# Conditioned residual convolution and expert mixing on one core: order of the opening loads, filler matmuls and the last unit's stores

## The chip, the cores and the metric

The kernel runs on one core of one Trainium2 chip. The metric is device time in microseconds of one execution; shown are the median and the limits of three runs. A profiled execution comes apart from these, with its own time and its span, which is the stretch from its first to its last recorded work.

## The reference, cut to what matters

```python
# x: (128, 64, 1024), cond_128: (128, 128)
def _L0_cond_ref(x, c, weight, c_weight, bias):
    ...
    out = lax.conv_general_dilated(x, weight, window_strides=(STRIDE,), padding=[(PAD, PAD)], dimension_numbers=('NCH', 'OIH', 'NCH'), feature_group_count=GROUPS)
    ctx = jnp.einsum('nd,od->no', c, c_weight)
    out = out + ctx[:, :, None] + bias[None, :, None]
    return out

def _L1_cond_ref(x, embedding, W0, b0, W1, b1, W2, b2, weight, bias_k):
    ...
    h = jax.nn.gelu(embedding @ W0 + b0, approximate=False)
    h = jax.nn.gelu(h @ W1 + b1, approximate=False)
    att = jax.nn.softmax((h @ W2 + b2) / T, axis=-1)
    agg_w = jnp.einsum('bk,koi->boi', att, weight[..., 0])
    agg_b = att @ bias_k
    out = jnp.einsum('boi,bih->boh', agg_w, x) + agg_b[:, :, None]
    return out
x = x + _L0_cond_ref(x, cond_128, L0_cond_weight, L0_cond_c_weight, fside_S_0)
x = x + _L1_cond_ref(x, cond_128, L1_cond_W0, L1_cond_b0, L1_cond_W1, L1_cond_b1, L1_cond_W2, L1_cond_b2, L1_cond_weight, L1_cond_bias_k)
```

Per sample: a grouped convolution of 9 taps over 64 channels with a residual, then a 64 x 64 matrix of its own, a softmax mixture of 8 expert matrices, again with a residual. Both residuals are folded into the matrices (the identity is added to them), all constants into one bias per sample and channel.

## The kernel before, in words

The 128 samples are worked in 16 units of 8 (NU, S). A unit u passes five stages.

- **Load.** SP and ScalarE each issue four DMAs (`load`, L195 and L285), one for each half of the length, into `xin[u % 2]`. Both queues run on the same 16 data engines.
- **Turn in.** VectorE transposes `xin` to `xph` (`turn_in`, L402), counted by `turned`. Unit 1 is turned in two parts (`second_phases`), with unit 0's first two column turns between them.
- **Convolution.** TensorE, `conv` (L528): four groups g, 12 matmuls each, into one half of PSUM tensor `yps`. Group 0 waits for `turned`, group g of unit 0 from g = 2 on for column turn g - 2 (`ycol_made`).
- **Turn back.** VectorE takes each group out of PSUM (`y_columns`, L424), and after four of them makes `ynat` (`y_natural`, L433).
- **Mixing.** TensorE, `mix` (L551): four pairs of samples o, into `zps`; ScalarE evacuates each with its bias (`evacuate`, L303) to `zout`, SP stores it (`store`, L199). `matrices` (L312) makes the unit's 64 x 64 matrices on ScalarE from `mixt`.

TensorE does unit u's groups 0 and 1, the pairs 0 and 1 of unit u - 1, groups 2 and 3, pairs 2 and 3. Every engine runs its own list in order; semaphores join them.

**The opening.** Inputs beside x: `mlps` (233.5 KB, all of the small network), `shares` (107 KB, identity and index patterns), `consts` (160 KB), `wraw` (208 KB, convolution), `mixw` (128 KB, experts). TensorE runs the network on 128 samples: L636 (first layer, h1 follows as Gelu on ScalarE, L328), L637 (for the bias), L639 (second layer, h2, L331), L642 and L643 (logits). VectorE takes the maximum, ScalarE exp (L333, which needs another function table than Gelu), GpSimd makes `att` (L247). L647 transposes it, ScalarE scales it four times (`attt`, L340). The aggregates (L509, 16 matmuls) mix the experts; they wait for `mixw` with GpSimd's identity added (L254, `mix_eye`). ScalarE's `gather` (L317) takes them out, four times. L623 makes the constants of the experts and waits for the first gather. conv(0) waits for two gathers, for `turned`, and for `w_sum`: `wraw` is doubled to the other 64 partitions (L443, VectorE, `w_both`), then GpSimd adds the residual (L257).

Between these steps TensorE multiplies a zeroed tile, a filler whose result nobody reads (`keep_on(n)`, L608; a matmul of it shows as two records): 4 at the very start, 3 ahead of L647, 3 ahead of the aggregates, 3 ahead of conv(0).

**The last unit.** Its group 3 is convolved in two halves of samples (`conv_last`, L565), turned back by quarters (L475, L482), each counted by `last_cols` and `last_nat`. Then `mix_first` (L577) makes pairs 0 and 2 whole, `mix_half` (L588) pairs 1 and 3 by halves of the length, ScalarE evacuates the first two in two instructions each (L379) and two halves (L385), VectorE the other two halves (L498). SP stores the two whole pairs (L226, 512 KB) and four halves (L229, 256 KB).

Of the kernel before, what the change touches and what calls it, by code (L numbers as in the profile page):

```python
# [42 lines left out]
def build(nc, x, conv_w, mlp, share, const_w, mix_w, out):  # L43
    ctx = ExitStack()
    with ctx:
# [725 lines left out]
```

## Time and profile before

| what | us |
|---|---|
| median of three runs | 248.84 |
| lowest, highest | 248.31, 249.13 |
| the profiled execution | 249.11 |
| its span | 247.3 |

| engine | busy us | share of the span |
|---|---|---|
| TensorE, matmul | 237.3 | 96% |
| VectorE | 220.3 | 89% |
| ScalarE | 126.6 | 51% |
| GpSimd | 10.4 | 4% |

All times in the profile are counted from the start of the span; the profiled execution took 1.8 us more than its span. DMA moved 68.39 MB, 277 GB/s on average. A row of the timeline gives start, duration, engine, line, operation, what is written from what is read, the count, and in brackets how long the engine stood idle before it and what released it. PE is TensorE's matmul, PEld its weight load, DVE is VectorE, ACT ScalarE, POOL GpSimd; SPq and ACTq are the issue of DMAs by SP and ScalarE.

### The profile page before, as it was taken

To read this page: it belongs to the slowest core of one execution; us is meant where nothing else is said; L and a number is where in the kernel's file an instruction comes from. 1 tells how busy PE (TensorE), PEld (TensorE's weight loads), DVE (VectorE), ACT (ScalarE), POOL (GpSimd) and SP (SyncE) were. 2 spreads that over 40 slices of the span, in tenths; PEclk is the share of its full clock that TensorE was granted. 3 is DMA by queue.
4 is the path that set the end of the run, shared out by engine and by line. 5 is a ranking of instruction groups with operands and counts; after the bars stand their busy time and mean duration, and the time that the engine had idled before them with its cause. 6 is when DMAs were issued, how large, how long until landed. Compare 5 with 4: busy or idle time off the path is not lost.

```text
span 247.3 us, 5763 instructions
## 1 busy us (share of the span) xinstructions
PE 237.3 (96%) x2162; PEld 103.9 (42%) x2162; DVE 220.3 (89%) x113; ACT 126.6 (51%) x208; POOL 10.4 (4%) x36
## 2 busy tenths in 40 slices
PE   6799999999999999999999999999999999999991
PEld 4643334344344444444444444444444444444530
DVE  1075899999999999999999999999999999999582
ACT  2457007374535456383645445373745446263772
POOL 1325000000000000000000000000000000000000
PEclk9689999999999999999999999999999999999999
DMA  7998566999999999999999999999999997444448
GB/s 189 307 326 240 152 125 191 258 312 365 357 322 268 359 263 383 249 380 238 334 294 292 327 256 378 247 388 239 362 273 322 298 281 293 170 170 172 171 184 328
DMA packets 28555, 68.39 MB, mean 277 GB/s; under 512 B 3184, under 2 KB 3568, under 8 KB 28544
## 3 DMA queue, kind: packets, MB, share of 16 engines
q1 hardware_dynamic: 19104, 50.98, 62.3%
q10 hardware_dynamic: 9440, 17.26, 26.5%
q8 instruction: 7, 0.11, 0.2%
q14 instruction: 4, 0.03, 0.0%
HBM read 34.67 MB, written 33.55 MB: 276 GB/s over the span
## 4 chain that ended last, share of the span: by engine, by line
PE 91%; DVE 3%; ACTq 2%; ACT 1%; issue 1%; DVEq 0%
PE yps L528 64%; PE zps L551 21%; PE yps L608 3%; DVE ynat L433 2%; ACTq L285 2%; PE yps L565 1%; PE zps L577 1%; DVE ycol L424 1%; PE yps L509 0%; PE yps L623 0%; PE yps L588 0%; ACT mixt L317 0%; DVE xin L498 0%; PE zps L588 0%; ACT L324 0%
## 5 line engine op out<-in xcount | busy, mean ns | idle before, releaser
L528 PE MATMUL yps<-xph,wraw 64*64 64x512 f32 x1512 | 169.0, 589 | 0.0
L303 ACT ACTIVATE zout<-zps,gamu 128x512 f32<-128x512 f32 x120 | 72.7, 688 | 95.3 <-PE zps L551 75.6
L528 PEld LDWEIGHTS yps<-xph,wraw 64*64 64x64 f32 x1512 | 67.5, 132 | 94.0 <-issue 94.0
L424 DVE STREAM_TRANSPOSE ycol<-yps 128x1024 f32<-128x1024 f32 x63 | 75.2, 1224 | 7.0 <-PE yps L528 5.4
L402 DVE STREAM_TRANSPOSE xph<-xin 128x4160 f32<-128x4160 f32 (+2 forms) x17 | 71.7, 4220 | 5.1 <-DMA xin<-in_x 5.1
L433 DVE STREAM_TRANSPOSE ynat<-ycol 128x4096 f32<-128x4096 f32 x15 | 66.7, 4446 | 1.1
L551 PE MATMUL zps<-ynat,mixv 64*64 64x512 f32 x480 | 57.8, 589 | 0.3 <-DVE ynat L433 0.3
L312 ACT ACTIVATE mixv<-mixt 64x256 f32 (+1 forms) x64 | 42.4, 663 | 1.4 <-ACT mixt L317 0.2
L551 PEld LDWEIGHTS zps<-ynat,mixv 64*64 64x64 f32 x480 | 21.6, 133 | 29.9 <-issue 29.6
L608 PE MATMUL yps<-zout 128*128 128x256 f32 x26 | 10.4, 566 | 1.3 <-POOL zout L243 1.3
L241 POOL COPY gamu<-gam 128x4 f32 (+1 forms) x16 | 2.9, 188 | 199.9 <-ACT zout L303 191.8
L608 PEld LDWEIGHTS yps<-zout 128*128 128x128 f32 x26 | 7.3, 296 | 3.2 <-POOL zout L243 1.3
L482 DVE STREAM_TRANSPOSE ynat<-ycol 128x1024 f32<-128x1024 f32 x4 | 4.7, 1224 | 0.1
L445 DVE TENSOR_REDUCE negmax<-zps 128x1 f32<-128x8 f32 x1 | 0.2, 167 | 4.0 <-PE zps L643 4.0
L351 ACT ACTIVATE gam<-zps 128x64 f32<-128x64 f32 x1 | 0.2, 224 | 6.8 <-PE zps L630 6.8
L324 ACT ACT_TABLE_LOAD x1 | 1.3, 1283 | 4.7 <-issue 4.7
L443 DVE COPY wraw<-wraw 64x832 f32<-64x832 f32 x1 | 0.6, 586 | 3.0 <-DMA wraw<-in_conv_w 3.0
L317 ACT ACTIVATE mixt<-yps 128x1024 f32<-128x1024 f32 x2 | 1.9, 1021 | 2.3 <-PE yps L509 2.3
L379 ACT ACTIVATE xin<-zps,gamu 128x512 f32<-128x512 f32 x4 | 2.4, 688 | 1.4 <-PE zps L577 1.4
L565 PE MATMUL yps<-xph,wraw 64*64 64x256 f32 x48 | 3.0, 375 | 0.0
L565 PEld LDWEIGHTS yps<-xph,wraw 64*64 64x64 f32 x48 | 2.2, 132 | 1.2 <-issue 1.0
L340 ACT ACTIVATE zout<-zps,shares 128x128 f32<-128x128 f32 x4 | 1.1, 368 | 2.5 <-PE zps L647 2.5
(56 smaller groups left out, 34.8 us busy)
## 6 DMA issues: line engine op xcount, KB each, us to landing
out<-zout SPq DMA_DIRECT2D x60, 512.0 KB, 6.2
xin<-in_x SPq DMA_DIRECT2D x64, 258.0 KB, 7.2
xin<-in_x ACTq DMA_DIRECT2D x64, 258.0 KB, 7.4
out<-xin SPq DMA_DIRECT2D x2, 512.0 KB, 2.7
out<-xin SPq DMA_DIRECT2D x4, 256.0 KB, 3.0
mlps<-in_mlp SPq DMA_DIRECT2D x1, 233.5 KB, 2.8
wraw<-in_conv_w ACTq DMA_DIRECT2D x1, 208.0 KB, 3.7
zout<-in_const_w SPq DMA_DIRECT2D x1, 160.0 KB, 9.3
```

The costliest lines, as they stand in the source:

```text
L241: nc.gpsimd.tensor_copy(gamu[slot][:], gam[:, bass.ds(PR * u, PR)]).then_inc(gam_cut, 1)
L285: act.dma_start(*x_piece(slot, u, 1, k, t)).then_inc(x_in[slot], 16)
L303: nc.scalar.activation(zout[:, o].rearrange("p (i c j q) -> p c i j q", i=2, c=2, q=PH)[:, c], zps[:, at:at + BANK].rearrange("p (q i j) - ...
L312: nc.scalar.activation(mix_places(slot, h, d), mix_values(u, d), ACT.Copy).then_inc(mixv_made, 1)
L402: nc.vector.transpose(xph[slot][:, :, :, at:to].rearrange("q g s j t -> q j s g t"), xin[slot][:, :, PH * at:PH * to].rearrange("q c (j p) ...
L424: nc.vector.transpose(ycol[:, :, :, :, :, g].rearrange("p i s j q c -> p (i s j) q c"), yps[:, 2 * BANK * (g % 2):2 * BANK * (g % 2) + 2 * ...
L433: nc.vector.transpose(ynat[slot][:].rearrange("p t q i s (j l) -> p (i s j) q t l", l=16), ycol[:].rearrange("p i s j q g c -> p (i s j q ...
L482: nc.vector.transpose(ynat[1][:, :, :, i, 2 * sh:2 * sh + 2].rearrange("p t q s (j l) -> p (s j) q t l", l=16), ycol[:, i, 2 * sh:2 * sh + ...
L528: last = nc.tensor.matmul(yps[C * c:C * c + C, at:at + BANK].rearrange("p (s f) -> p s f", s=S // 2), wsum[rows, b, g], xph[slot][rows, g, ...
L551: last = nc.tensor.matmul(zps[C * s:C * s + C, at:at + BANK].rearrange("p (n j) -> p n j", j=NJ), mixv[slot][rows, 2 * o + s], ynat[slot][ ...
L565: last = nc.tensor.matmul(y_last(sh)[C * c:C * c + C, i].rearrange("p (s f) -> p s f", s=2), wsum[rows, b, G - 1], xph[1][rows, G - 1, 2 * ...
L608: nc.tensor.matmul(yps[:, 3 * BANK:3 * BANK + BANK // 2], still[:, 0:P], still[:, 0:BANK // 2], start=True, stop=True)
```

## The change

- SP no longer issues `shares`; ScalarE does, as its first DMA. `wraw` and `mixw` are issued by ScalarE behind h1 instead of ahead of x(0), `mixw` first. The Gelu table and the warm-up instruction stand ahead of load(0). Of x(1)'s four pieces on ScalarE two are issued behind h1, two behind `beta`.
- The copy of `wraw` to the other partitions goes from VectorE to ScalarE, behind `attt` and ahead of the first gather. GpSimd adds the constants' identity ahead of the sum over `wraw`.
- Filler: one matmul behind L637 and one behind L639 are added, the three ahead of the aggregates become five, the three ahead of conv(0) go.
- The last unit is mixed, evacuated and stored in eight halves of a pair, in the order of a table, `LAST`. ScalarE evacuates six, VectorE two.

```diff
+LAST = (0, 0), (2, 0), (0, 1), (2, 1), (1, 0), (3, 0), (1, 1), (3, 1)
...
         def z_half(o, i):
 
-            return (yps, zps)[i][:, BANK * (o - 1):BANK * (o - 1) + 2 * BANK].rearrange(
-                "p (c h f) -> p h c f", c=2, h=2)[:, 0]
+            bank, at = {(0, 0): (zps, 0), (2, 0): (yps, 2), (0, 1): (zps, 2), (2, 1): (zps, 0),
+                        (1, 0): (yps, 0), (3, 0): (yps, 2), (1, 1): (zps, 2), (3, 1): (zps, 0)}[o, i]
+            return bank[:, BANK * at:BANK * at + 2 * BANK].rearrange("p (c h f) -> p h c f", c=2, h=2)[:, 0]
...
             sp.dma_start(mlps[:], mlp).then_inc(mlp_in, 16)
-            sp.dma_start(shares[:], share).then_inc(share_in, 16)
             load(0, 0)
...
-            for o in (0, 2):
-                sp.wait_ge(z_act, o + 2)
-                sp.dma_start(z_rows(NU - 1, o), out_last(o)).then_inc(z_out[o], 16)
-            for o, i, made, n in ((1, 0, z_act, 5), (1, 1, z_dve, 1), (3, 0, z_act, 6), (3, 1, z_dve, 2)):
-                sp.wait_ge(made, n)
+            for n, (o, i) in enumerate(LAST):
+                sp.wait_ge(z_act if n < 6 else z_dve, n % 6 + 1)
                 sp.dma_start(z_rows(NU - 1, o)[:, H * i:H * i + H], out_half(o, i)).then_inc(z_out[o], 16)
...
-            pool.wait_ge(w_both, 1)
-            nc.gpsimd.tensor_tensor(wsum[:, 1], wsum[:, 1], wraw[:, NT * G:].broadcast_to([P, G, C]),
-                                    ALU.add).then_inc(w_sum, 1)
             pool.wait_ge(const_in, 16)
...
+            pool.wait_ge(w_both, 1)
+            nc.gpsimd.tensor_tensor(wsum[:, 1], wsum[:, 1], wraw[:, NT * G:].broadcast_to([P, G, C]),
+                                    ALU.add).then_inc(w_sum, 1)
...
-            act.dma_start(wraw[0:C], conv_w).then_inc(w_in, 16)
-            act.dma_start(mixw, mix_w).then_inc(mix_in, 16)
-            load(0, 0)
+            act.dma_start(shares[:], share).then_inc(share_in, 16)
             act.wait_ge(zeroed, 1)
             nc.scalar.activation(warm[:], warm[:], ACT.Gelu)
-            load_block(1, 1, 0)
+            load(0, 0)
             act.wait_ge(mlp_in, 16)
             act.wait_ge(mm, 1)
             nc.scalar.activation(h1, sps[:, 0:NS], ACT.Gelu, bias=b0s).then_inc(act_mlp, 1)
-            load_block(1, 1, 1)
+            act.dma_start(mixw, mix_w).then_inc(mix_in, 16)
+            act.dma_start(wraw[0:C], conv_w).then_inc(w_in, 16)
+            load_block(1, 1, 0)
...
+            load_block(1, 1, 1)
             act.wait_ge(share_in, 16)
             act.wait_ge(mm, 4)
             for o in range(RO):
                 nc.scalar.activation(attt[:, o], sps[:, 0:NS], ACT.Copy, scale=turn[:, o:o + 1]).then_inc(soft, 1)
+
+            act.wait_ge(w_in, 16)
+            nc.scalar.activation(wraw[C:P], wraw[0:C], ACT.Copy).then_inc(w_both, 1)
             gather(0, 1, 4)
...
-            dve.wait_ge(w_in, 16)
-            nc.vector.tensor_copy(wraw[C:P], wraw[0:C]).then_inc(w_both, 1)
...
             nc.tensor.matmul(gps[0:C, 0:NS], cws, condt, start=True, stop=True).then_inc(beta_mm, 1)
+            keep_on(1)
             pe.wait_ge(act_mlp, 1)
             nc.tensor.matmul(sps[:, NS:2 * NS], w1s, h1, start=True, stop=True).then_inc(mm, 1)
+            keep_on(1)
...
             keep_on(3)
+            keep_on(2)
             aggregates()
             output_constants()
-            keep_on(3)
...
             pe.wait_ge(mixv_made, 4 * NU)
+            pe.wait_ge(last_nat, 1)
+
+            pe.wait_ge(z_made, 8 * NU - 10)
+            mix_half(0, 0)
+
+            pe.wait_ge(last_cols, 2)
+            mix_half(2, 0)
             pe.wait_ge(last_nat, 2)
 
-            pe.wait_ge(z_made, 8 * NU - 10)
-            mix_first(0)
-
             pe.wait_ge(z_made, 8 * NU - 8)
-            mix_first(2)
+            mix_half(0, 1)
+
+            pe.wait_ge(z_act, 1)
+            mix_half(2, 1)
             pe.wait_ge(last_nat, 3)
-
             pe.wait_ge(last_cols, 4)
             mix_half(1, 0)
+            pe.wait_ge(z_act, 2)
             mix_half(3, 0)
             pe.wait_ge(last_nat, 4)
-
-            pe.wait_ge(z_act, 2)
+            pe.wait_ge(z_act, 3)
             mix_half(1, 1)
-
             pe.wait_ge(z_act, 4)
             mix_half(3, 1)
```

ScalarE's list in the opening: as it was, up to `beta`, and as it is now, from load(0), which stands behind `shares`, the table and the warm-up, to the copy of `wraw` (the first zout activation is h1, the second h2, the four are attt):

```order
L320 DMA wraw<-in_conv_w 64x832
L321 DMA zout<-in_mix_w 128x256
L285 DMA xin<-in_x 16x8x516 x4
L324 ACT_TABLE_LOAD
L324 ACTIVATE warm<-warm 128x1
L285 DMA xin<-in_x 16x8x516 x2
L328 ACTIVATE zout<-zps,mlps 128x128
L285 DMA xin<-in_x 16x8x516 x2
L331 ACTIVATE zout<-zps,mlps 128x128
L333 ACT_TABLE_LOAD
L333 ACTIVATE expv,esum<-zps,negmax 128x8
L336 ACTIVATE beta<-zps,mlps 64x128
```

```order
L280 DMA xin<-in_x 16x8x516 x4
L321 ACTIVATE zout<-zps,mlps 128x128
L322 DMA zout<-in_mix_w 128x256
L323 DMA wraw<-in_conv_w 64x832
L280 DMA xin<-in_x 16x8x516 x2
L326 ACTIVATE zout<-zps,mlps 128x128
L328 ACT_TABLE_LOAD
L328 ACTIVATE expv,esum<-zps,negmax 128x8
L331 ACTIVATE beta<-zps,mlps 64x128
L280 DMA xin<-in_x 16x8x516 x2
L336 ACTIVATE zout<-zps,shares 128x128 x4
L339 ACTIVATE wraw<-wraw 64x832
```

h1 has no table load right ahead of it any more, and four DMA issues stand between h1 and h2 where two stood. The copy of `wraw` is new, ahead of gather.

TensorE's list up to the first convolutions, before and now (yps<-zout 128x256 is the filler, the 64x512 rows are the aggregates, yps<-zout,beta is L623):

```order
L636 MATMUL zps<-mlps 128x128
L637 MATMUL zps<-mlps 64x128
L639 MATMUL zps<-zout,mlps 128x128
L642 MATMUL zps<-mlps,zout 128x8
L643 MATMUL zps<-mlps,ones 128x8
L608 MATMUL yps<-zout 128x256 x3
L647 MATMUL zps<-shares,att 128x128
L608 MATMUL yps<-zout 128x256 x3
L509 MATMUL yps<-zout 64x512 x8
L509 MATMUL zps<-zout 64x512 x8
L623 MATMUL yps<-zout,beta 128x512
L608 MATMUL yps<-zout 128x256 x3
```

```order
L612 MATMUL zps<-mlps 64x128
L583 MATMUL yps<-zout 128x256
L615 MATMUL zps<-zout,mlps 128x128
L583 MATMUL yps<-zout 128x256
L619 MATMUL zps<-mlps,zout 128x8
L620 MATMUL zps<-mlps,ones 128x8
L583 MATMUL yps<-zout 128x256 x3
L624 MATMUL zps<-shares,att 128x128
L583 MATMUL yps<-zout 128x256 x5
L495 MATMUL yps<-zout 64x512 x8
L495 MATMUL zps<-zout 64x512 x8
L598 MATMUL yps<-zout,beta 128x512
```

The filler moved from the place ahead of the convolution to places between the network's layers and ahead of the aggregates.

## Rows read from the trace of the kernel before

**Rows 1.** The page's chain, by engine.

```profile
PE 91%; DVE 3%; ACTq 2%; ACT 1%; issue 1%; DVEq 0%
```

**Rows 2.** The chain in order of time, the start: start us, us, what.

```profile
9.01 2.86 PE yps L608 x6
...
19.43 10.52 PE yps L528 x96
...
35.85 1.95 PE zps L551 x16
```

**Rows 3.** Slices of 1 us, the opening, from 6 us on.

```profile
core 0: us, PE busy (x) PEld busy (x) DVE busy (x) ACT busy (x) POOL busy (x), PEclk, DMA share, GB/s
...
6.00:7.00 1.00, 0.47 (x2) 0.30 (x2) 0.00 (x0) 0.48 (x2) 0.00 (x0) 1.00 0.97 281
...
7.00:8.00 1.00, 0.10 (x2) 0.11 (x1) 0.00 (x0) 0.57 (x2) 0.00 (x0) 0.80 1.07 287
...
8.00:9.00 1.00, 1.00 (x5) 0.95 (x5) 0.00 (x0) 1.00 (x1) 0.00 (x0) 0.50 1.07 235
...
14.00:15.00 1.00, 1.00 (x10) 0.36 (x17) 1.00 (x1) 0.00 (x0) 0.91 (x1) 0.79 1.05 349
```

**Rows 4.** Timeline of the opening.

```profile
4.54 0.38 PE L636 MATMUL zps<-mlps 128*128 128x128 f32 x2
...
4.67 1.28 ACT L324 ACT_TABLE_LOAD   x1 [4.67 <-issue]
...
6.12 1.24 ACTq L285 DMA_DIRECT2D xin<-in_x  x2
...
7.41 0.37 ACT L331 ACTIVATE zout<-zps,mlps 128x128 f32<-128x128 f32 x1 [0.93 <-PE zps L639]
...
9.90 0.60 POOL L247 TENSOR_SCALAR att<-expv,erec 128x128 f32<-128x128 f32 x1 [8.48 <-DVE erec L447]
...
13.64 1.27 POOL L261 TENSOR_TENSOR zout<-zout,shares 64x512 f32<-64x512 f32 x1 [1.74 <-DMA zout<-in_const_w]
...
17.04 1.10 PE L623 MATMUL yps<-zout,beta 80*128 80x512 f32 x2 [0.43 <-ACT mixt L317]
...
17.97 1.46 PE L608 MATMUL yps<-zout 128*128 128x256 f32 x6
...
18.67 1.02 ACT L317 ACTIVATE mixt<-zps 128x1024 f32<-128x1024 f32 x1
```

**Rows 5.** Timeline of VectorE, 12 to 37 us.

```profile
13.03 4.51 DVE L402 STREAM_TRANSPOSE xph<-xin 128x4160 f32<-128x4160 f32 x1 [3.23 <-DMA xin<-in_x]
...
19.37 2.38 DVE L402 STREAM_TRANSPOSE xph<-xin 128x2112 f32<-128x2112 f32 x1 [1.83 <-DMA xin<-in_x]
...
22.24 1.25 DVE L424 STREAM_TRANSPOSE ycol<-yps 128x1024 f32<-128x1024 f32 x1 [0.49 <-PE yps L528]
```

**Rows 6.** Issues of x by ScalarE at 3.96 and 4.73, and at 6.74.

```profile
xin<-in_x ACTq DMA_DIRECT2D x2, 258.0 KB, 9.3
...
xin<-in_x ACTq DMA_DIRECT2D x1, 258.0 KB, 12.2
```

**Rows 7.** The tail: timeline, a slice of 1 us, the landing of L229's stores.

```profile
235.15 2.37 DVE L482 STREAM_TRANSPOSE ynat<-ycol 128x1024 f32<-128x1024 f32 x2
...
237.62 1.95 PE L577 MATMUL zps<-ynat,mixv 64*64 64x512 f32 x16 [0.47 <-issue]
...
238.85 2.42 ACT L379 ACTIVATE xin<-zps,gamu 128x512 f32<-128x512 f32 x4 [1.38 <-PE zps L577]
...
240.15 1.49 SPq L226 DMA_DIRECT2D out<-xin  x2
...
240.00:241.00 1.00, 0.97 (x20) 0.36 (x12) 0.59 (x1) 1.00 (x3) 0.00 (x0) 1.00 0.05 20
...
241.88 2.56 SPq L229 DMA_DIRECT2D out<-xin  x4
...
DMA to landing us min/median/max: 2.9/3.0/3.2
```

More of the change, by code:

```diff
@@ L159, in y_last @@
                 "p (i h f) -> p h i f", i=2, h=2)[:, 0]
-        def z_first(o):
-            return zps[:, BANK * o:BANK * o + 2 * BANK].rearrange("p (c f) -> p c f", c=2)
         def z_half(o, i):
-            return (yps, zps)[i][:, BANK * (o - 1):BANK * (o - 1) + 2 * BANK].rearrange(
-                "p (c h f) -> p h c f", c=2, h=2)[:, 0]
+            bank, at = {(0, 0): (zps, 0), (2, 0): (yps, 2), (0, 1): (zps, 2), (2, 1): (zps, 0),
+                        (1, 0): (yps, 0), (3, 0): (yps, 2), (1, 1): (zps, 2), (3, 1): (zps, 0)}[o, i]
+            return bank[:, BANK * at:BANK * at + 2 * BANK].rearrange("p (c h f) -> p h c f", c=2, h=2)[:, 0]
         def out_last(o):
@@ L223, in _ @@
                     store(u, o)
-            for o in (0, 2):
-                sp.wait_ge(z_act, o + 2)
-                sp.dma_start(z_rows(NU - 1, o), out_last(o)).then_inc(z_out[o], 16)
-            for o, i, made, n in ((1, 0, z_act, 5), (1, 1, z_dve, 1), (3, 0, z_act, 6), (3, 1, z_dve, 2)):
-                sp.wait_ge(made, n)
+            for n, (o, i) in enumerate(LAST):
+                sp.wait_ge(z_act if n < 6 else z_dve, n % 6 + 1)
                 sp.dma_start(z_rows(NU - 1, o)[:, H * i:H * i + H], out_half(o, i)).then_inc(z_out[o], 16)
             for o in range(PR):
-                sp.wait_ge(z_out[o], 16 * NU + 16 * (o % 2))
+                sp.wait_ge(z_out[o], 16 * NU + 16)
         @block.gpsimd
@@ L376, in _ @@
             act.wait_ge(turned, NU)
-            def evacuate_first(o, c):
-                nc.scalar.activation(
-                    out_last(o).rearrange("p (i c j q) -> p c i j q", i=2, c=2, q=PH)[:, c],
-                    z_first(o)[:, c].rearrange("p (q i j) -> p i j q", q=PH, i=2),
-                    ACT.Identity, bias=gamu[1][:, o:o + 1]).then_inc(z_act, 1)
             def evacuate_half(o, i):
@@ L388, in evacuate_half @@
                     ACT.Identity, bias=gamu[1][:, o:o + 1]).then_inc(z_act, 1)
-            for o in (0, 2):
-                act.wait_ge(last_mixes, 1 + o // 2)
-                for c in range(2):
-                    evacuate_first(o, c)
-            for o in (1, 3):
-                act.wait_ge(last_mixes, 3 + o // 2)
-                evacuate_half(o, 0)
+            for n, (o, i) in enumerate(LAST[:6]):
+                act.wait_ge(last_mixes, n + 1)
+                evacuate_half(o, i)
         @block.vector
@@ L495, in _ @@
             dve.wait_ge(gam_cut, NU)
-            for n, o in enumerate((1, 3)):
-                dve.wait_ge(last_mixes, 5 + n)
+            for n, (o, i) in enumerate(LAST[6:]):
+                dve.wait_ge(last_mixes, 7 + n)
                 nc.vector.tensor_scalar(
-                    out_half(o, 1).rearrange("p (c j q) -> p c j q", c=2, q=PH),
-                    z_half(o, 1).rearrange("p c (q j) -> p c j q", q=PH),
+                    out_half(o, i).rearrange("p (c j q) -> p c j q", c=2, q=PH),
+                    z_half(o, i).rearrange("p c (q j) -> p c j q", q=PH),
                     gamu[1][:, o:o + 1], None, ALU.add).then_inc(z_dve, 1)
@@ L570, in conv_last @@
                 last.then_inc(last_conv, 1)
-            def mix_first(o):
-                for c in range(2):
-                    rows = slice(C * c, C * c + C)
-                    for s in range(2):
-                        last = nc.tensor.matmul(
-                            z_first(o)[C * s:C * s + C, c].rearrange("p (n j) -> p n j", j=NJ), mixv[1][rows, 2 * o + s],
-                            ynat[1][rows, o // 2, :, :, s].rearrange("p q i j -> p (q i) j"),
-                            start=True, stop=True)
-                last.then_inc(last_mixes, 1)
             def mix_half(o, i):
@@ L589, in mix_half @@
                             z_half(o, i)[C * s:C * s + C, c].rearrange("p (n j) -> p n j", j=NJ),
-                            mixv[1][rows, 2 * o + s], ynat[1][rows, o // 2, :, i, 2 + s],
+                            mixv[1][rows, 2 * o + s], ynat[1][rows, o // 2, :, i, 2 * (o % 2) + s],
                             start=True, stop=True)
```

## The prediction

> **What bounds the kernel now.** I read the page's chain first [rows 1]: 91% of it is TensorE, so what counts is when TensorE's unbroken stretch begins and what follows it. The chain in order of time [rows 2] gives the beginning: the first convolution starts at 19.43 us, unit 0's four groups run 10.52, so 2.63 each, and the first mixing is at 35.85. From there TensorE alternates without a gap, and a shift of 35.85 shifts everything behind it. So the change has two parts: the start, up to 35.85, and the tail behind the last mixing.
>
> In the start three things end close together. First TensorE's own time filler, L608: it is on the chain at 9.01 for 2.86 us, and it runs from 17.97 to 19.43, straight ahead of conv(0). The early ones ran at half clock: six filler records took 2.86 then and 1.46 at the end [rows 2, 4]. The granted clock is 1.00 in the slice from 6, 0.80 in that from 7, 0.50 in that from 8 and 0.79 in that from 14, which puts the fall at 7.6 and the rise at 14.4; TensorE was busy 0.47 and 0.10 of the two slices at the fall [rows 3]. Second, VectorE turns x of unit 0 from 13.03 for 4.51 us, on the arrival of its last piece. Third, it turns x of unit 1 from 19.37, again on the arrival [rows 5].
>
> **The start, edit by edit.**
> *Order of transfers.* On ScalarE's queue wraw (208 KB) and mixw (128 KB) stood ahead of x(0); now only the shares (107 KB) do, 229 KB less. Pieces of 258 KB landed on this queue at 3.96 + 8.9 = 12.9 us (the 9.3 of the row is the median of two issues, the other landing later) and, four pieces on, at 6.74 + 12.2 = 18.9: 1.5 us each, about 170 KB/us [rows 6]. So x(0) lands 1.4 earlier, 11.6 instead of 13.0, and its turn ends at about 16.1 instead of 17.5. Mixw then lands near 12.3 and wraw near 13.6; SP's const_w, which GpSimd took up at 13.64 [rows 4], comes some 0.6 earlier. The bytes up to the end of x(1) are the same, and the data engines moved 235 to 349 GB/s throughout [rows 3], so x(1) hardly moves: the two queues are better balanced, and I take 19.2 for 19.37.
>
> *Gelu table first.* The load (1.28 us at 4.67) ended at 5.95 while the matmul for h1 was through at 4.92 [rows 4]. It now runs from 1.35, and h1 can begin at 5.0 instead of 6.1. But behind h1 ScalarE's queue now issues mixw, wraw and two pieces of x before it comes to h2. Two pieces took 1.24 [rows 4], so four issues take 2.5, and h2 starts at 7.6; before it was 7.41 [rows 4]. **The table's gain is given back to four DMA issues**: this edit alone is worth 0 to -0.2.
>
> *Filler.* One matmul of it now stands behind L637 and one behind L639, both where TensorE would wait; three stay ahead of L647, five replace three ahead of the aggregates, none stands ahead of conv(0). What this costs hangs on the clock. **If it stays full** (case A): from the end of h2 to the filler it was 1.2 us (7.78 to 9.01), at full clock some 0.3 less, but exp waits for its table until 7.97 + 1.28 = 9.3 anyway, where before it was 9.25. Att was made at 10.50 [rows 4] and is again, L647 is through at 11.0, and five fillers, ten records at 0.243, end at 13.4. By then ScalarE's four attt (each like h2's 0.37, so 1.5 at most) and mixw with GpSimd's adds (12.3 and under 1 us: att took it 0.60 for as many elements) are ready. The aggregates start at 13.4 instead of 14.65, the end of the fillers before. From there to the end of L623 it was 3.5, up to 18.14 [rows 4], and nothing follows it now, so conv(0) can start at 16.9. **If it falls at 7.6 as before** (case B): the fillers ahead of L647 end at 12.1, five more begin at 12.5, four records run at 0.47 until 14.4, six at 0.243, and the aggregates start at 15.9, 1.2 later: conv(0) at 19.3, a gain of 0.1.
>
> *The copy of wraw from VectorE to ScalarE, behind attt.* ScalarE has no row for 64x832: between h2's 0.37 for 128 elements a partition and 1.02 for 1024 [rows 4], and by the length near 0.88. It runs from 13.6 to 14.5, just ahead of gather, whose matmuls are then through at 14.6: hidden by them, with 0.1 to spare. A wraw that lands later pushes gather and conv(0) one for one. GpSimd's constant add now comes first (1.27, done by 14.4), then its sum over wraw (under 1 us, by 15.4): hidden until 16.9.
>
> *What is late next.* Group 2 of conv(0) needs the first column turn, which VectorE does behind x(1): 19.2 + 2.38 + 1.25 [rows 5] and two handovers, 23.0. Before, group 2 began at 19.43 + 5.26 = 24.69. So the gain is capped at 1.7, and reached if conv(0) starts by 17.7: case A has 0.8 to spare. From group 2 to the mixing it was 11.2, and the order there is the old one: mixing at 34.2.
>
> **The tail.** Before, the first mixing of the last unit waits for both halves of ynat (235.15 + 2.37) and takes 1.95 for two pairs; ScalarE starts at 238.85, and the first store issues at 240.15, behind two evacuations. The data engines are nearly empty from 240 to 241 (20 GB/s), and the last four stores issue from 241.88 over 2.56 us, the last at 243.8 and landing 3.0 later at 246.9 [rows 7]. About 2.1 MB are to be written behind 240.9; at 5.4 us for them, which is 385 GB/s, data end at 246.3, so this is bound by bandwidth. Now the first step is half a pair (1.95 / 4, 0.5 us). It needs ynat's first half (236.4) and TensorE, which is free at 237.15 (0.47 idle before 237.62). ScalarE starts at 237.9, each evacuation 0.61, the first store issues at 238.65 and seven more 0.64 apart, to 243.2. The last half of ynat is made at 240.6, the last pair at 241.7, and VectorE's two evacuations are ahead of SP's turn for them. The data engines are busy with the unit before until 239.75, then have 2.1 MB without a break: 5.5 us, to 245.2 instead of 246.3, **1.05 earlier**. By issue and landing it is 243.2 + 3.0 = 246.2 instead of 246.9, 0.7. I take 1.05, since the engines' bandwidth is the nearer bound, and keep 0.6 to 1.3.
>
> The Trainium skill (DMA: Bandwidth & Descriptors, Anatomy of one DMA) gives a DMA some 2.0 us fixed plus its bytes at 436 GB/s, fitted on GpSimd's path: 2.6 us for a half. By it, as an estimate, 243.2 + 2.6 would give 1.1 for the tail; the trace's 3.0 gives 0.7.
>
> **Sum.** Case A: 1.7 + 1.05 = 2.75. The profiled execution took 249.11, 0.27 over the median of 248.84; against the median it is 246.1. Case B: 0.1 + 1.05, that is 247.7.
>
> **Rivals.**
> *B, the clock falls anyway.* For it: the two fillers still leave TensorE idle from 6.7 to 8.0. Against: the gap ahead of L639 is closed. 247.7.
> *C, the gap freed ahead of conv(0) costs the clock (slower).* Without the last fillers TensorE idles around L623, and if the clock then falls, conv(0) runs at half rate. The one fall in the trace lasted 6.8 us, 3.4 us of work. From A's 16.9 group 2 then begins at 25.6, which the tail makes even; from B's 19.3 at 28.0, 3.3 late, less 1.05: 251.1. It decides where the clock is 0.50 from 19 us on. Against it: TensorE idled 0.43 ahead of L623 before [rows 4] and the clock held.
> The Trainium skill (TensorE: Matmul & The Clock Gate, What's actually happening) calls throttled the default that activity releases; by it filler taken out is a risk, and the fall at 7.6 agrees.
> *D, wraw comes late.* It is now the last of the matrices on ScalarE's queue, and its copy holds gather. At 15 us conv(0) starts at 18, at 16.5 at 19.4, and the start's gain is gone: 247.8. The steady landing rate speaks against it.
> *E, the tail gives nothing,* if half rows are slower to write or the issues bind: A becomes 247.1, B 248.7, no change.
> *F, x(1) comes later than before,* since its last two pieces are issued only behind exp, at 9.6: at 20.1 A becomes 247.0. The queue has work until 15, so I give it little.
>
> **How the numbers follow.** A 0.45 (246.1), B 0.28 (247.7), D 0.07 and F 0.05 (247 to 247.8), E 0.09 (half of it no change), C 0.06. The likeliest is A, 246.2 with 0.1 for small handovers. The range goes from A with a tail of 1.3 and x(1) 0.4 earlier, 245.4, to B with a tail of 0.6, 248.2. A measurement of this kernel can tell 0.3% from no change, 0.75 us, so faster means under 248.1: A, D, F, most of B and half of E, 0.82; no change 0.12; slower 0.06.
>
> **What would show it.** For A: granted clock 1.00 from 8 to 13 us, aggregates at 13.4, conv(0) at 16.9, its group 2 at 23.0 straight behind the first column turn, mixing at 34.2. In every case h2 at 7.6, right behind the issues. In the tail: stores 0.64 apart and no empty slice in the data engines. If h2 comes before 7.2 or conv(0) after 19.4, my account of the start is wrong; if, measured from the last unit's mixing, data end less than 0.6 earlier, that of the tail is.

## The result and the profile after

The changed kernel takes **250.53 us** (median of 18 runs, 249.04 to 252.40) where the kernel before, run beside it, takes 248.64. The ratio is 1.008, interval 1.006 to 1.010: **slower by 1.9 us**. The forecast was 246.2 with a range up to 248.2, so it was wrong, in sign too. The profiled execution took 250.66, against 249.11 before: 1.55 us more. In some sets one execution stands far apart (422.17 us among the 18 of the kernel before, 644.53 among the twelve of t6 below), and the ratios leave it out.

The page's chain answers to [rows 1]: TensorE has fallen from 91% to 84%, and 5% of the path is now a load of x.

```profile
PE 84%; DVE 6%; DMA 5%; ACTq 1%; ACT 1%; issue 0%; DVEq 0%; POOL 0%; POOLq 0%
```

The chain in order of time (start, us, what) answers to [rows 2] and says which load:

```profile
10.15 13.26 DMA xin<-in_x
...
23.43 2.38 DVE xph L391
25.81 1.14 DVE ycol L413
...
27.09 5.42 PE yps L514 x48
...
33.82 4.46 DVE ynat L422
...
38.41 1.95 PE zps L537 x16
```

ScalarE's last piece of x(1), issued at 10.15, lands at 23.4. Its turn in, the first column turn and conv(0)'s group 2 follow without a gap, and the first mixing stands at 38.41 where it was 35.85. That is 2.56 us lost in the start. From there the order is the old one.

The timeline of the opening answers to [rows 4, 5]:

```profile
5.62 0.37 ACT L321 ACTIVATE zout<-zps,mlps 128x128 f32<-128x128 f32 x1 [2.95 <-PE zps L611]
...
6.63 1.42 ACTq L280 DMA_DIRECT2D xin<-in_x  x2
8.10 0.37 ACT L326 ACTIVATE zout<-zps,mlps 128x128 f32<-128x128 f32 x1 [2.12 <-issue]
...
11.48 2.32 PE L583 MATMUL yps<-zout 128*128 128x256 f32 x10
16.90 1.12 PE L495 MATMUL yps<-zout 32*64 32x512 f32 x16 [3.10 <-POOL zout L249]
...
20.30 5.39 PE L514 MATMUL yps<-xph,wraw 64*64 64x512 f32 x48
27.09 5.39 PE L514 MATMUL yps<-xph,wraw 64*64 64x512 f32 x48 [1.40 <-DVE ycol L413]
...
14.30 4.51 DVE L391 STREAM_TRANSPOSE xph<-xin 128x4160 f32<-128x4160 f32 x1 [3.97 <-DMA xin<-in_x]
23.43 2.38 DVE L391 STREAM_TRANSPOSE xph<-xin 128x2112 f32<-128x2112 f32 x1 [4.62 <-DMA xin<-in_x]
...
16.00 0.76 POOL L249 TENSOR_TENSOR zout<-zout,shares 128x16 f32<-128x16 f32 x4 [4.96 <-DMA zout<-in_mix_w]
...
17.18 0.90 ACT L339 ACTIVATE wraw<-wraw 64x832 f32<-64x832 f32 x1 [4.30 <-DMA wraw<-in_conv_w]
```

Every load on ScalarE's queue behind x(0)'s third piece lands later than forecast: x(0) is complete at 14.3, mixw at 15.8 (GpSimd waits 4.96 us for it), wraw at 17.1 (ScalarE waits 4.30), x(1) at 23.4. The matrices were not issued late: mixw and wraw were issued at 5.6 and 6.0 and landed 10.2 and 11.1 us on. The last piece of x(1) was, at 10.15 instead of 6.74; run t7 below tests that. The issues of x(0)'s third and fourth piece by ScalarE, 2.85 and 3.5 us into the span, in the view of DMAs (KB, us to landing), answer to [rows 6]:

```profile
xin<-in_x ACTq DMA_DIRECT2D x1, 258.0 KB, 7.7
...
xin<-in_x ACTq DMA_DIRECT2D x1, 258.0 KB, 10.7
```

That is 10.5 and 14.2, a step of 3.7 us where the two steps before are 2.0 and 1.6. The slices of 1 us (columns as in [rows 3]) show the data engines at that time:

```profile
10.00:11.00 1.00, 0.78 (x4) 0.35 (x2) 0.16 (x1) 0.39 (x3) 0.56 (x1) 1.00 1.05 324
11.00:12.00 1.00, 0.81 (x5) 0.79 (x6) 0.00 (x0) 0.26 (x1) 0.04 (x1) 1.00 1.09 246
12.00:13.00 1.00, 1.00 (x7) 0.87 (x6) 0.00 (x0) 0.89 (x4) 0.00 (x0) 1.00 1.12 220
13.00:14.00 1.00, 0.81 (x4) 0.38 (x2) 0.00 (x0) 0.00 (x0) 0.00 (x0) 1.00 1.06 211
14.00:15.00 1.00, 0.00 (x0) 0.00 (x0) 0.70 (x1) 0.00 (x0) 0.00 (x0) 1.00 1.05 205
...
19.00:20.00 1.00, 0.72 (x2) 0.30 (x2) 0.00 (x0) 1.00 (x2) 0.00 (x0) 1.00 1.07 225
```

The last two columns are the share in which the data engines were busy, and what they moved. The share stays at 1.05 to 1.12 whether they move 324 or 205 GB/s: **a full share is not a full rate**. Before, the same slices were these, with the fourth in [rows 3]:

```profile
11.00:12.00 1.00, 1.00 (x5) 0.82 (x4) 0.00 (x0) 0.00 (x0) 0.91 (x3) 0.50 1.07 352
12.00:13.00 1.00, 1.00 (x5) 0.82 (x4) 0.00 (x0) 0.61 (x3) 0.00 (x0) 0.50 1.08 291
13.00:14.00 1.00, 1.00 (x4) 0.82 (x3) 0.97 (x1) 0.53 (x3) 0.35 (x1) 0.50 1.04 324
```

So the four slices from 11 us moved 352, 291, 324 and 349 GB/s, and now move 246, 220, 211 and 205, which is 0.43 MB less. From 19 to 20 ScalarE's queue runs all but alone, 0.20 of 0.22 MB, at 225. In the changed kernel the granted clock (the column before the share) is 1.00 in all of these.

The tail, timeline and slices, answers to [rows 7]:

```profile
240.78 2.37 DVE L468 STREAM_TRANSPOSE ynat<-ycol 128x1024 f32<-128x1024 f32 x2
...
240.99 4.95 SPq L224 DMA_DIRECT2D out<-xin  x8
...
242.08 1.09 PE L563 MATMUL yps<-ynat,mixv 64*64 64x256 f32 x16 [0.40 <-DVE ynat L468]
```

```profile
240.00:241.00 1.00, 1.00 (x20) 0.49 (x12) 0.97 (x4) 0.76 (x3) 0.00 (x0) 1.00 0.99 401
...
245.00:246.00 1.00, 0.00 (x0) 0.00 (x0) 0.42 (x1) 0.00 (x0) 0.00 (x0) 1.00 1.00 371
...
247.00:248.00 1.00, 0.00 (x0) 0.00 (x0) 0.00 (x0) 0.00 (x0) 0.00 (x0) 0.95 0.84 320
```

From 240 us on the data engines no longer pause: they write 371 to 406 GB/s in every full slice, until 247.85. The old end, 246.3, moved by the 2.56 of the start would be 248.86: the tail gives 1.0 us. And 2.56 - 1.0 is the 1.55 between the profiled executions.

### The profile page after: what moved, and what is told of

It reads as the page before. It is cut to its first block, busy times and chain, and to the rows that moved or that the text cites. A ratio compares the mean times of both kernels' runs of the same rounds, so it can differ in the third digit from the quotient of the medians.

```text
span 248.9 us, 5802 instructions
## 1 busy us (share of the span) xinstructions
PE 235.6 (95%) x2180; PEld 103.2 (41%) x2180; DVE 219.4 (88%) x112; ACT 127.6 (51%) x209; POOL 10.5 (4%) x36
## 4 chain that ended last, share of the span: by engine, by line
PE 84%; DVE 6%; DMA 5%; ACTq 1%; ACT 1%; issue 0%; DVEq 0%; POOL 0%; POOLq 0%
PE yps L514 61%; PE zps L537 20%; DMA xin<-in_x 5%; DVE ynat L422 2%; PE yps L583 2%; DVE ynat L468 1%; DVE ycol L413 1%; DVE xph L391 1%; ACTq L280 1%; DVE ycol L461 1%; PE yps L551 1%; ACT L328 1%; PE yps L563 0%; DVE xin L484 0%; PE zps L563 0%
## 5 line engine op out<-in xcount | busy, mean ns | idle before, releaser
L583 PE MATMUL yps<-zout 128*128 128x256 f32 x28 | 9.0, 465 | 1.3 <-POOL zout L238 1.3
L583 PEld LDWEIGHTS yps<-zout 128*128 128x128 f32 x28 | 6.0, 230 | 2.3 <-POOL zout L238 1.3
L495 PE MATMUL yps<-zout 32*64 32x512 f32 x16 | 1.1, 611 | 3.1 <-POOL zout L249 3.1
L339 ACT ACTIVATE wraw<-wraw 64x832 f32<-64x832 f32 x1 | 0.9, 896 | 4.3 <-DMA wraw<-in_conv_w 4.3
L563 PE MATMUL zps<-ynat,mixv 64*64 64x256 f32 x40 | 3.0, 386 | 0.0
L484 DVE TENSOR_SCALAR xin<-zps,gamu 128x512 f32<-128x512 f32 x2 | 1.4, 746 | 0.9 <-PE zps L563 0.9
L563 PE MATMUL yps<-ynat,mixv 64*64 64x256 f32 x24 | 1.7, 384 | 0.4 <-DVE ynat L468 0.4
## 6 DMA issues: line engine op xcount, KB each, us to landing
wraw<-in_conv_w ACTq DMA_DIRECT2D x1, 208.0 KB, 11.1
zout<-in_mix_w ACTq DMA_DIRECT2D x1, 128.0 KB, 10.2
```

What stands on the lines that cost most here:

```text
L563: last = nc.tensor.matmul(z_half(o, i)[C * s:C * s + C, c].rearrange("p (n j) -> p n j", j=NJ), mixv[1][rows, 2 * o + s], ynat[1][rows, o ...
L583: nc.tensor.matmul(yps[:, 3 * BANK:3 * BANK + BANK // 2], still[:, 0:P], still[:, 0:BANK // 2], start=True, stop=True)
```

## The experiments

These were the theories before the first run. **Place**: the matrices now stand in the midst of x on ScalarE's queue, and what is behind them lands late. **Issue**: ScalarE issues them too late. **Clock**: some executions lose TensorE's clock in the new idle stretches. Ratios are to the kernel before on the same chip, whose median was 248.8.

### The parts of the change

t1 is the kernel before with the changed last unit alone. 

> The kernel before with the changed tail alone (eight halves of a pair); its opening is the old one. In the changed kernel the data end 1.0 us earlier, measured from the last unit's third turn back (L468 at 240.78 there, L482 at 238.22 before), so both theories of the start expect 247.6 +-0.2 here. A tail that gives nothing would leave 248.6; then the loss of the start would be only about 1.9 us instead of 2.9.

Measured 247.84, ratio 0.997 (0.9954 to 0.9986). The tail is a gain of 0.3 to 1.1 us.

t2 is the changed kernel with the old last unit. 

> The changed kernel with the old tail. If the two parts add, the opening costs 250.5 - 248.6 + 1.0 = 2.9 us, and this runs 251.5, with runs spread over some 3 us as those of the changed kernel are. x of unit 1 should be turned from about 23 us, as in the changed kernel's profile (23.43), not from 19.4. If it came out near 248.6 the loss would sit in the tail or in both together.

Measured 252.07, 1.012 (1.011 to 1.014): the start alone costs 3.3 us. In its profile, which is of the slowest of its five runs (254.84), x(0) is complete at 15.07, x(1) at 24.16, and the clock is lost besides (0.50 from 17 to 27 us).

t3 is t1 with the changed filler too, every load and ScalarE's list as before:

```diff
+            keep_on(1)
             pe.wait_ge(act_mlp, 1)
...
+            keep_on(1)
...
             keep_on(3)
+            keep_on(2)
             aggregates()
             output_constants()
-            keep_on(3)
```

> The kernel before with the changed filler matmuls and the changed tail; the order of all loads, the function table and the copy of wraw stay as they were. Both theories of the loads (place of the small matrices; late issue of x(1)'s last pieces) expect x(1) at 19.4 here. With the clock held at full, TensorE's aggregates start by 13.5 instead of 14.65, conv(0) waits for the turn of x(0) at 17.6, group 2 starts at 23.1 instead of 24.7: 247.6 - 1.6 = 246.0. If the clock falls at 7.6 as before, conv(0) is at 19.3 and the time 247.5. If the lost filler costs the clock at conv(0), over 249.

Measured 247.66 (247.37 to 248.18), 0.9948 (0.9934 to 0.9963); the clock is 1.00 from the start. My case A for the filler holds, yet it is worth only 0.2 beyond t1, and their intervals overlap, since conv(0) cannot use it. Its timeline:

```profile
13.27 1.11 PE L495 MATMUL yps<-zout 32*64 32x512 f32 x16
...
18.11 5.39 PE L514 MATMUL yps<-xph,wraw 64*64 64x512 f32 x48 [1.34 <-DVE xph L388]
24.18 5.39 PE L514 MATMUL yps<-xph,wraw 64*64 64x512 f32 x48 [0.68 <-DVE ycol L410]
```

Aggregates come at 13.27 (the forecast's 13.4), but conv(0) then waits for x(0)'s turn in, group 2 for x(1)'s. TensorE is no longer what binds the start; x is. And x varies from one execution to another: with the same loads in the same order x(1) is turned from 19.37 in the profile of the kernel before, 20.14 in t1's and 20.52 here. In the changed kernel's order of loads it is 22.63 in t8's profile, 23.43 in its own and 24.16 in t2's. So a difference in x(1) of 1.5 us or less between two profiles shows little.

### Place or issue

t4 is the changed kernel with both matrices back ahead of load(0), behind the shares:

```diff
             act.dma_start(shares[:], share).then_inc(share_in, 16)
+            act.dma_start(mixw, mix_w).then_inc(mix_in, 16)
+            act.dma_start(wraw[0:C], conv_w).then_inc(w_in, 16)
...
-            act.dma_start(mixw, mix_w).then_inc(mix_in, 16)
-            act.dma_start(wraw[0:C], conv_w).then_inc(w_in, 16)
             load_block(1, 1, 0)
```

> The changed kernel with mixw and wraw issued ahead of load(0) again (behind the shares and the table); x(1)'s last two pieces are still issued only behind exp. Theory place: the slow stretch of the data engines at 11 to 15 us (205 to 246 GB/s) comes from the matrices' rows in the midst of x, and goes with them: x(1) back at 19.4 to 20, conv(0) at 17.7, total 246 to 246.5. Theory late issue: x(1) stays at 22 to 23 because two pieces are issued at 9.5 and 10.2, total 249 to 250.5.

Measured 250.50, 1.0062 (1.0039 to 1.0085): by the time alone, no cure, and what the theory of late issue had forecast. Its timeline says otherwise:

```profile
20.31 2.38 DVE L391 STREAM_TRANSPOSE xph<-xin 128x2112 f32<-128x2112 f32 x1 [1.09 <-DMA xin<-in_x]
...
19.47 12.24 PE L514 MATMUL yps<-xph,wraw 64*64 64x512 f32 x96 [2.89 <-DVE xph L391]
```

x(1) is complete 3.1 us earlier than in the changed kernel, and the slices of 14 to 18 us move 361 to 365 GB/s: **the place of the two matrices was the cause of the late x(1)**. x(0) is no earlier than in the changed kernel (turned from 14.70 instead of 14.30). TensorE idles 2.89 us ahead of conv(0), which waits for that turn, and then the clock falls:

```profile
20.00:21.00 1.00, 1.00 (x14) 0.36 (x10) 0.69 (x1) 0.00 (x0) 0.83 (x3) 0.81 0.16 45
21.00:22.00 1.00, 1.00 (x12) 0.47 (x8) 1.00 (x1) 0.00 (x0) 0.00 (x0) 0.50 0.96 293
...
23.00:24.00 1.00, 1.00 (x8) 0.33 (x4) 0.17 (x1) 0.97 (x2) 0.00 (x0) 0.50 0.96 213
```

u1 is t4 with that gap filled, six matmuls of filler ahead of conv(0)'s wait:

```diff
+            keep_on(6)
             pe.wait_ge(w_sum, 1)
```

> The kernel with both matrices ahead of load(0), and six filler matmuls (12 records at 0.243, 2.9 us) put back ahead of conv(0), where its profile shows TensorE idle for 2.89 us and the granted clock at half from 19.6 us. If the clock is what that kernel lost after its x(1) came back at 20.3, conv(0) starts at 19.4 at full clock, the granted clock over the span is 0.997 or more, and the time 248.2 to 248.8 instead of 250.5. If the clock is no cause it stays within 0.3 of 250.5.

Measured 248.28 (248.06 to 248.74), 0.9976 (0.9963 to 0.9989). The timeline has no fall:

```profile
19.39 10.54 PE L514 MATMUL yps<-xph,wraw 64*64 64x512 f32 x96 [0.61 <-DVE xph L391]
```

All 96 matmuls take 10.54 us, where they took 12.24 in t4. So what t4 gained by its loads, some 2.2 us, it had lost again to the clock, by rival C's mechanism: an idle stretch ahead of conv(0). It takes both edits to gain it: the matrices' place alone gives 250.50 (t4), more filler in the changed kernel alone 250.44 (t8 below), place and filler together 248.28.

t5 puts wraw alone ahead of load(0), t6 mixw alone. 

> The changed kernel with wraw alone back ahead of load(0) on ScalarE's queue; mixw stays behind h1, between x(0) and x(1). Theory place, wraw's part: the 3.7 us between the third and the fourth piece of x(0) (10.5 and 14.2 in the changed kernel, 1.6 apart elsewhere) and the slow stretch come from wraw; they go, mixw lands by 14, x(1) is at 20. Theory place, mixw's part: the gap stays at 3 us or more, mixw lands at 15 to 16 and x(1) at 22 to 23. In both the time depends on the clock as well: below 249.5 if mixw lands by 14, 250 to 251 otherwise.

> The mirror image: mixw back ahead of load(0), wraw behind h1. Theory wraw's part: the gap ahead of the fourth piece of x(0) stays at 3 us, wraw lands at 16 to 17, gather and conv(0) follow it, x(1) is at 22 to 23 and the time 250 to 251. Theory mixw's part: no gap, wraw lands at 14, x(1) at 20, time below 249.5. The aggregates start at 13.4 in either case, since mixw is there.

t5 measured 250.92, 1.0094 (1.0054 to 1.0135); t6 249.03, or 248.49 without the one at 644.53, and 1.0006 (0.9983 to 1.003). In both x(0)'s fourth piece still lands at 14.5, 2.8 and 3.7 us behind the third. It does not take both matrices behind it. x(1) comes at 21.65 and 21.23, between t4 and the changed kernel. The times differ by the clock. In t5's profile the aggregates wait 4.24 us for mixw and run at half clock, in t6's they start at 13.14; six of t5's eight runs have a mean clock of 0.982 or less and took 250.8 us or more, and its two at 0.993 took 248.9 and 249.1, where t6's four at 0.993 took 248.4 to 250.0.

t7 issues x(1)'s last two pieces behind the first two, at once:

```diff
             load_block(1, 1, 0)
+            load_block(1, 1, 1)
             act.wait_ge(mm, 2)
...
-            load_block(1, 1, 1)
             act.wait_ge(share_in, 16)
```

> The changed kernel with x(1)'s last two pieces on ScalarE issued right behind its first two, ahead of h2. Theory place: nothing gets better, x(1) at 23 to 24, the chain of the network 1.3 us later (h2 at 9.4), hidden since mixw comes at 15.8 anyway: 250.5 +-0.5. Theory late issue: x(1) back at 20 to 21, time 248.5 to 249.

Measured 249.94, 1.0047 (1.0023 to 1.0071). x(1) is still only complete at 23.74, against 23.43. The theory of the late issue falls. Why the median is 0.6 lower is not shown; the intervals overlap.

### Is it the clock?

t8 gives the changed kernel ten matmuls of filler ahead of the aggregates in place of five. 

> The changed kernel with ten filler matmuls instead of five ahead of the aggregates, so that TensorE is busy to 16.4 us and mixw (15.8) is hardly held up. If part of the loss is the clock, which fell between 16 and 26 us in one of two profiles, the slow half of its runs (251 to 252.4) goes: median 249.6, spread below 1.5 us, granted clock over the span 0.997 or more. If the loss is all in the loads, the median stays at 250.3 to 250.7.

Measured 250.44 (248.56 to 251.79), 1.0064 (1.0039 to 1.009), with a mean granted clock of 0.995 or more in all twelve runs. The clock is kept, and median and spread stay, 1.6 us above the kernel before. The clock costs t4 2.2 us, but it is not what makes the changed kernel slower.

### What makes the loads slow

SP's pieces of x go to partitions 0 to 63, ScalarE's to 64 to 127 (one half of the length each, `x_places`). wraw goes to 0 to 63, mixw to all. The theory of the **halves** is that the engines reach 350 GB/s only while the two queues write different halves. u2 loads wraw to 64 to 127 and turns the copy round:

```diff
-            act.dma_start(wraw[0:C], conv_w).then_inc(w_in, 16)
+            act.dma_start(wraw[C:P], conv_w).then_inc(w_in, 16)
...
-            nc.scalar.activation(wraw[C:P], wraw[0:C], ACT.Copy).then_inc(w_both, 1)
+            nc.scalar.activation(wraw[0:C], wraw[C:P], ACT.Copy).then_inc(w_both, 1)
```

> The changed kernel with wraw loaded to partitions 64 to 127 instead of 0 to 63, and the copy in the other direction. SP's pieces of x go to partitions 0 to 63, ScalarE's to 64 to 127. Theory halves (a half of the partitions takes only some 200 to 225 GB/s, the rate seen whenever one queue runs alone): wraw no longer shares SP's half, the rate at 13 to 15 us rises from 205 to 300 or more, wraw lands 1 us earlier, x(1) at 22 or earlier, time 249.5. Theory small rows (matrices are slow wherever they go): no change, 250.5 +-0.4.

Measured 249.47, 1.0014 (0.9996 to 1.0033): 1.1 us better for one address. Slices:

```profile
12.00:13.00 1.00, 1.00 (x7) 0.87 (x6) 0.00 (x0) 1.00 (x4) 0.00 (x0) 1.00 1.10 256
13.00:14.00 1.00, 0.99 (x5) 0.54 (x3) 0.04 (x1) 0.07 (x1) 0.00 (x0) 1.00 1.05 298
14.00:15.00 1.00, 0.00 (x0) 0.00 (x0) 1.00 (x1) 0.00 (x0) 0.00 (x0) 1.00 1.03 309
```

They move 256, 298 and 309 where the changed kernel has 220, 211 and 205, t8 225, 222 and 197, and t2 241, 201 and 216, the last two with the changed kernel's loads. x(1) is turned from 21.76, earlier than in all three. (This profile is of the slowest of its twelve runs, with the clock at 0.50 from 18 to 24 us; the loads are read from it, not the time.)

u3 takes t3, whose loads are the old ones, and cuts x between the queues the other way, so that each queue writes both halves in turn:

```diff
-                    for t in range(2):
-                        sp.dma_start(*x_piece(slot, u, 0, k, t)).then_inc(x_in[slot], 16)
+                    for i in range(2):
+                        sp.dma_start(*x_piece(slot, u, i, k, 0)).then_inc(x_in[slot], 16)
...
-                for t in range(2):
-                    act.dma_start(*x_piece(slot, u, 1, k, t)).then_inc(x_in[slot], 16)
+                for i in (1, 0):
+                    act.dma_start(*x_piece(slot, u, i, k, 1)).then_inc(x_in[slot], 16)
```

> The kernel before with changed filler and tail (247.66), and x cut between the queues by t instead of by the half of the length, so that each queue writes both halves of the partitions in turn. Theory halves: when one queue runs alone it alternates, and the two queues no longer use complementary halves for certain; the rate with both at work may fall from 350, and a queue alone rises above 225. Either sign of the time is open, 246.5 to 249.5; what tells is the rate in the slices where one queue moves nearly all bytes: 200 to 225 means a limit of the queue, over 260 a limit of the half.

Measured 251.29, 1.0082 (1.0057 to 1.0107): 3.6 us over t3, with the same bytes, pieces and issues. x(1) is complete at 24.87 instead of 20.52, and conv(0)'s group 2 and the first mixing follow as much later. In step the two queues would still write different halves, but they are not in step: SP's pieces of x(0) land at 7.95, 10.35, 12.53 and 14.55, ScalarE's at 9.18, 11.70, 13.75 and 15.51. Two of its slices, and then those of t3:

```profile
11.00:12.00 1.00, 1.00 (x6) 0.92 (x7) 0.00 (x0) 0.45 (x2) 1.00 (x5) 1.00 1.03 266
...
16.00:17.00 1.00, 0.00 (x0) 0.00 (x0) 1.00 (x1) 0.72 (x1) 0.56 (x1) 1.00 1.12 244
```

```profile
11.00:12.00 1.00, 1.00 (x7) 0.90 (x6) 0.00 (x0) 0.72 (x3) 0.98 (x3) 1.00 1.07 347
...
16.00:17.00 1.00, 0.77 (x2) 0.00 (x0) 1.00 (x1) 0.64 (x2) 0.00 (x0) 1.00 1.06 326
```

From 10 to 22 us u3's slices have 227 to 281 GB/s. None of them has one queue alone, so the sign that its expectation named, a limit of the queue or of the half, is not there to read. The tail of the changed kernel has it, for stores: from 241 to 246 us SP's queue is alone and moves 1.92 MB from all 128 partitions, 384 GB/s.

```profile
q1 hardware_dynamic: 920, 1.92, 100.8%
```

In t5's two slices from 22 us SP's queue is alone too, loads one half of the partitions and moves 200 and 206 GB/s. So a queue as such can move more than that, at least when it stores.

u3 also changes which samples the two queues read at one time. v1 keeps the halves apart and changes only that, `for t in (1, 0)` on ScalarE. 

> The kernel before with changed filler and tail (247.66), ScalarE's pieces of x in the order t = 1, 0 instead of 0, 1, so that the two queues are on different samples but still in complementary halves of the partitions. Theory halves: nothing changes, 10 to 17 us keep 320 to 350 GB/s, x(1) at 20 to 20.5, 247.7 +-0.4. Theory rows: the rate falls to 250 as in the cut by t, x(1) at 24 or later, over 250.

Measured 247.76, 0.9964 (0.9939 to 0.9989), level with t3, and the same two slices are near t3's:

```profile
11.00:12.00 1.00, 0.59 (x4) 0.50 (x4) 0.00 (x0) 0.00 (x0) 1.00 (x5) 1.00 1.04 353
...
16.00:17.00 1.00, 0.15 (x9) 0.10 (x1) 1.00 (x1) 1.00 (x2) 0.84 (x1) 1.00 1.03 334
```

x(1) comes at 21.24, later than the 20 to 20.5 expected and well short of u3's 24.87. It is the halves written, not the samples read, that cost u3 its rate.

The Trainium skill (SBUF — State Buffer, Door 1: The DMA port swizzle) says that partitions 0 to 63 reach one half of the memory's 16 ports and 64 to 127 the other, about 218 GB/s each. The traces agree within 10%: the slices in which one queue wrote one half all but alone have 225 in the changed kernel and 200 and 206 in t5. The same page ("Can I just issue two DMAs to hit both halves?") answers no and gives two such DMAs 6% over one. The rows here speak against that: 326 to 367 GB/s with two queues on their own halves, 200 to 225 with one.

### What the rest of the start costs

v5 is the changed kernel with the shares back on SP's queue; u4 has them there and the table and warm-up behind load(0) too.

```diff
             sp.dma_start(mlps[:], mlp).then_inc(mlp_in, 16)
+            sp.dma_start(shares[:], share).then_inc(share_in, 16)
...
-            act.dma_start(shares[:], share).then_inc(share_in, 16)
```

> The changed kernel with only the shares back on SP; the table stays first. If the shares' way back makes the 1.2 us gain of both together, this runs 249.3; if the table's place does, it runs 250.5; a mere order of issue with x(0) on ScalarE's queue 0.6 us ahead of SP's would sit between.

> The changed kernel with the shares on SP again and the Gelu table behind load(0) again; the two matrices stay behind h1, the copy of wraw on ScalarE, the filler and the tail as changed. If the matrices' place alone makes the loss, it stays: 250.0 to 250.9, the last piece of x(0) on ScalarE's queue over 3 us behind the third, x(1) at 23. If the shares on ScalarE's queue or the table have a part of it, the time falls below 249.7.

v5 249.14, 1.0009 (0.999 to 1.0028); u4 249.31, 1.0014 (0.999 to 1.0038). The shares' new place costs 1.4 us, the table's nothing that shows. How the shares cost it is open: v5's profile has x(1) at 23.10, hardly earlier than the changed kernel's 23.43, but that profile is of its slowest run (250.32). In u4 ScalarE's fourth piece of x(0) does not land over 3 us behind the third, as expected from the matrices behind it, but 1.6; in v5 it is 1.8. There SP's fourth piece is the late one, 2.4 and 2.8 us behind its third.

v2 is u4 with wraw in the upper half. 

> The changed kernel with shares on SP and the table behind load(0) again (249.31 alone) and wraw in the upper half of the partitions (249.47 alone; the changed kernel 250.5). If the two gains are of different origin they add: 248.3 to 248.6. If both only cure the same loss, it stays at 249.2 to 249.5.

Measured 248.76, 1.0013 (0.9994 to 1.0033). By the medians the two cures give 1.2 and 1.1 alone and 1.8 together. The ratios of u4, u2 and v2 are all but the same (1.0014, 1.0014, 1.0013), and 248.76 lies between the two forecasts, so whether they add is not shown. Nor do the gains of single edits add up to the start's loss: the shares back give 1.4, mixw back 1.5 to 2.0 (t6), both matrices with filler 2.2, and all of it together, which is t3, 2.9.

v4 is t3 with wraw, still the first transfer, in the upper half. 

> The kernel before with changed filler and tail, and wraw, the first transfer of ScalarE's queue, to the upper half. At 1 to 5 us SP moves mlps and shares, which reach all partitions. Theory halves: wraw lands up to 0.5 us earlier, x(0) and x(1) by as much at most, 247.3 to 247.7. Nothing in the theory of small rows changes: 247.66 +-0.2.

Measured 247.59 (246.44 to 249.61), 0.9967 (0.9938 to 0.9997). The slices of 4 to 6 us move 297 and 308 GB/s (t3 has 248 and 248), and x(1) comes 0.6 earlier in its profile, but the kernel before has 291 and 237 there with the old address and x(1) earlier still, so neither shows a gain. The median is t3's and the spread wider. **The best version is t3**, 247.66: 1.1 us under the kernel before and 2.9 under the change.

## Why the prediction was wrong

**The step that failed** is the first: "The bytes up to the end of x(1) are the same, and the data engines moved 235 to 349 GB/s throughout [rows 3], so x(1) hardly moves: the two queues are better balanced, and I take 19.2 for 19.37." It was 23.4. I counted bytes and took their rate as given. The bytes were the same and the issue times did not matter (t7); the rate fell from about 330 to 220 GB/s for four microseconds, because the matrices in the midst of x broke up the pairing of the queues. That their place does it is shown by t4, that the half which wraw writes is a part of it by u2; for mixw, which writes both halves, the pairing is an inference. The row of 235 was already in [rows 3], and I read past it. From the same step hang x(0) at 11.6 (it was 14.3), mixw at 12.3 (15.8) and wraw at 13.6 (17.1). Group 2 was to start 3.8 behind x(1)'s landing, at 23.0; it started 3.7 behind, at 27.09. The first mixing is then 38.41 instead of 34.2: 4.2 of the 4.4 us between 246.1 and 250.5. The prediction had named a sign for this, conv(0) after 19.4, and it came true at 20.30.

**Rivals D and F** named the right loads but the wrong causes and sizes. D put wraw at 16.5 at most as bad and gave it 0.07; it came at 17.1 and conv(0) at 20.30, and even so it did not bind, for x(1) came later still. F had x(1) at 20.1 by late issue; t7 shows that the issue is not the cause. "The steady landing rate speaks against it" was the same error: the rate was steady because the order was. C's 251.1 lies nearest to what was measured, but mostly by luck: in the changed kernel's profile the clock is at 1.00 throughout conv(0), and t8, which keeps the clock in every run, takes as long. B did not happen in the profiles of the change and of t3, and E is refuted by t1.

**Right by the steps:**
- *Four issues give the table's gain back.* h1 went from 6.11 to 5.62 only (I had 5.0; L611 began at 4.88 and took 0.63), h2 came at 8.10, straight behind the issues; I had 7.6. u4 and v5 are level, so the edit is worth nothing that shows.
- *The clock, case A.* 1.00 from 8 to 13 us in the profiles of the change and of t3. The fillers ended at 13.8 (13.4). But the medians of t3 and t1 differ by 0.2: TensorE is ready early and nothing comes of it while x binds.
- *The cost of the copy*: 0.90 (0.88).
- *The tail*: 1.0 us in the profile (1.05), with stores back to back; t1 has 0.75 by the ratio, 0.95 by the medians.
- *Rival C*: its mechanism exists (t4 to u1, 2.2 us), as an idle stretch ahead of conv(0) that costs the clock; in the changed kernel it does not set the median (t8).

**What stays open.** Why ScalarE's fourth piece of x(0) lands 2.8 to 3.7 us behind its third in t5, t6 and the changed kernel. That a matrix follows it on the queue is not enough: with mixw behind it, it landed 2.5 behind in t8, 1.8 in v5, 1.6 in u4 and 1.5 in v2, and in v1, with a piece of x behind it, 2.5. Why mixw, which writes all partitions, does as much as wraw; that its rows are small (1 KB a partition) was not tried apart. That the queues' halves matter is shown, how the engines share them is not. What of the shares' 1.4 us is halves and what a longer queue was not separated. The changed kernel's runs spread over 3.4 us. Those with a mean clock of 0.986 lie at 250.5 to 252.4, those of 0.996 and more at 249.0 to 251.2, so the clock is a part of it; t8 keeps the clock and spreads as far, and what else varies was not found.

## What to carry to other kernels

Before a transfer is moved in a queue, look at which partitions it and its neighbours on the other queue write: 128 KB to 208 KB in the wrong place cost more here than their bytes, and a data engine's busy share of 1.05 hid it. The rate in slices of 1 us shows it. When an experiment changes the loads, fill the new idle time of TensorE too, or the clock may hide the answer, as in t4. And try the parts of a change one by one: here the tail and the filler together were worth keeping (1.1 us) and the order of transfers was not.

## What was not expected of the hardware

- The rate of 16 busy data engines was 326 to 367 GB/s with each queue on its own half of the partitions (t3, t4, the changed kernel), 227 to 281 with both queues alternating between halves (u3), 200 to 225 with one queue on one half (t5, the changed kernel).
- A piece of x on ScalarE's queue with a matrix behind it landed 3.7 us behind its forerunner in the changed kernel, where 1.6 is usual, but 1.6 behind in u4, where SP's queue was behind ScalarE's.
- TensorE idled 3.10 us ahead of the aggregates of the changed kernel and its clock held at 1.00. In t5 it idled 4.24 us there, and the clock was at 0.50 from 15 to 21 us. In t4 it idled 2.89 us ahead of conv(0), and the clock was at 0.50 from 21 to 24 us.
- Stores of half a row moved 371 to 406 GB/s back to back, on one queue.
